# Weights of a quantised feed-forward rounded on VectorE inside an earlier stage, its input rows normalised by two engines

## What is computed

```python
# routed feed-forward, layer 0: top 3 of 64 experts, 128 places each
buf = zeros.at[fe, pos].set(xf[tok])                       # gather rows by expert
h = gelu(einsum('ecd,edh->ech', buf, w1) + b1)
y = einsum('ech,ehd->ecd', h, w2) + b2
out = zeros.at[tok].add(y[fe, pos] * gate)                 # scatter-add

# quantised feed-forward, layer 1: w_up, w_gate (768, 256), w_down (256, 768)
def lpbq_dequant(w):                                       # blocks of 32 along a row
    s = max(max|wb| / 7, 1e-12)
    return clip(round(wb / s), -8, 7) * s
x = act_qdq(x)                                             # one scale for all of x
up, gate = act_qdq(x @ dequant(w_up).T), act_qdq(x @ dequant(w_gate).T)
o = act_qdq(act_qdq(gate * fixed(sigmoid(gate))) * up)
out = o @ dequant(w_down).T
```

## Time and profile before

| | us |
|---|---|
| median of 3 runs (lowest, highest) | 2735.41 (2733.01, 2735.60) |
| the profiled execution, its own time | 2738.86 |
| its span in the profile | 2737.10 |
| mean granted clock of TensorE | 0.921 |
| DMA over the span | 339.40 MB, mean 124 GB/s |

### The profile page before, as it was taken

How to read it: one execution, slowest core, us unless ns; L and a number is a source line. 1 busy time by engine, 2 the same in 40 slices (tenths; PEclk the granted TensorE clock), 3 DMA queues, 4 the chain that set the end, 5 groups by cost and what they waited for, 6 DMA issues and landing times. The chain is left out here.

```text
span 2737.1 us, 52948 instructions
## 1 busy us (share of the span) xinstructions
PE 2340.4 (86%) x18240; PEld 1860.6 (68%) x18240; DVE 1495.7 (55%) x2887; ACT 1247.6 (46%) x2737; POOL 629.3 (23%) x690
## 2 busy tenths in 40 slices
PE   8989999877999999489948999999999997695047
PEld 5669999767999999478835666666666665353035
DVE  5766666574111111268844666565666664644865
ACT  2223323211434343168734656555555654436753
POOL 1101111155434444534431121111121110000000
PEclk9999999968999999789968999999999997798579
DMA  2122322082999999500025555555455551110111
GB/s 81 53 72 70 78 71 65 22 281 81 341 342 345 341 348 342 174 1 0 0 45 135 128 125 125 128 122 122 119 128 125 125 125 48 59 57 0 50 46 42
DMA packets 375990, 339.40 MB, mean 124 GB/s; under 512 B 70227, under 2 KB 351853, under 8 KB 374637
## 3 DMA queue, kind: packets, MB, share of 16 engines
q1 hardware_dynamic: 311148, 294.82, 36.5%
q10 hardware_dynamic: 52480, 26.83, 3.9%
q0 software_dynamic: 12288, 16.79, 2.8%
HBM read 255.03 MB, written 83.37 MB: 124 GB/s over the span
## 5 line engine op out<-in xcount | busy, mean ns | idle before, releaser
L2124 ACT COPY rel_probT<-rel_ps_t 121x400 f32<-121x400 f32 x384 | 196.4, 511 | 259.5 <-PE rel_ps_t L2356 259.5
L2136 ACT ACTIVATE rel_prob<-rel_ps_s,rel_nmx 100x361 f32<-100x361 f32 x512 | 264.9, 580 | 2.1 <-DVE rel_nmx L2238 2.1
L2356 PEld LDWEIGHTS rel_ps_t<-rel_ident,rel_prob 100*121 100x121 f32 x1536 | 197.7, 187 | 78.1 <-ACT rel_probT L2124 49.2
L2356 PE MATMUL rel_ps_t<-rel_ident,rel_prob 100*121 100x100 f32 x1536 | 244.5, 282 | 7.2 <-ACT rel_probT L2124 7.2
L1328 PEld LDWEIGHTS moe_ps_h<-moe_xeT,moe_w 128*128 128x128 f32 x2048 | 241.3, 194 | 5.1 <-issue 1.9
L1328 PE MATMUL moe_ps_h<-moe_xeT,moe_w 128*128 128x128 f32 x2048 | 241.9, 277 | 1.3 <-DVE moe_xeT L1493 1.3
L2238 DVE TENSOR_REDUCE rel_nmx<-rel_ps_s 100x2 f32<-100x722 f32 x256 | 232.8, 909 | 8.8
L1328 PE MATMUL moe_ps_y<-moe_w,moe_hT 128*128 128x256 f32 x1024 | 231.4, 379 | 0.0
L1319 ACT ACTIVATE moe_hT<-moe_ps_h,moe_b 128x128 f32<-128x128 f32 x512 | 143.0, 375 | 138.4 <-PE moe_ps_h L1328 138.0
L2876 PE MATMUL ffd_ps_y<-ffn_w_dT,ffd_oq 128*100 128x256 f32 x384 | 85.9, 385 | 140.2 <-DVE ffd_oq L2821 134.6
L1328 PEld LDWEIGHTS moe_ps_y<-moe_w,moe_hT 128*128 128x128 f32 x1024 | 189.6, 190 | 23.2
(11 more groups left out here) (430 smaller groups left out, 4946.2 us busy)
## 6 DMA issues: line engine op xcount, KB each, us to landing
moe_w<-in_L_ffn_w SPq DMA_DIRECT2D x128, 1024.0 KB
rel_scores<-rel_r_ext SPq DMA_DIRECT2D x32, 818.8 KB
rel_r_key<-rel_scores SPq DMA_DIRECT2D x32, 818.8 KB
rel_weights<-rel_prob ACTq DMA_DIRECT2D x128, 204.7 KB
rel_by_dist<-rel_weights SPq DMA_DIRECT2D x32, 400.0 KB
mut_ctx_nat<-in_ctx SPq DMA_DIRECT2D x32, 363.0 KB
mut_ctx_T<-in_ctxT SPq DMA_DIRECT2D x16, 722.0 KB
rel_ctx_T<-in_ctxT SPq DMA_DIRECT2D x32, 361.0 KB, 3.3
```

The costliest lines, as they stand in the source:

```text
L2124: nc.scalar.copy(probT[:, pg % 2, c], ps_pT).then_inc(s_t_sb, 1)
L2136: last = nc.scalar.activation(prob[:, t.parity, slot, :], ps_s[0:S, j, 0:L], ACT.Exp, bias=nmx[:, slot:slot + 1])
L2356: last = nc.tensor.transpose(ps_pT[:, j, :], prob[:, pt.parity, QUAD * pg + j, c * STEP:c * STEP + R], ident[0:S, 0:S])
```

## The change

- A new class `QuantisedAhead` owns the three weight tiles, for which memory is now held from the routed stage to the end. Its `load` puts the three loads on SP's queue at the head of the routed stage, behind `ahead.load`. Its `step` issues one of 18 instructions: six for each tile, the same operations as before, each waiting for the one before it.
- DVE's list for the experts: the loop ends at expert 42 instead of 62, the last 22 are written out, and one step follows each of experts 42 to 59.
- POOL adds the first two one-hots straight into `mask`; the tile `hot01` goes.
- Preparation stage: no loads and no quantising. DVE normalises the rows of the first three groups (12 sequences) and takes their maxima, then takes the maxima of the other five as ACT finishes them, and copies the three transposes of the down weights out of PSUM (three banks of their own) after the first three of these. ACT normalises 20 rows, written out without the loop, and copies the 8 transposes of the up and gate weights. PE makes the first four of those, then the three of the down weights, then the last four.
- `up_kept` gets its memory behind this stage.

```diff
+class QuantisedAhead:
+    STEPS = 18
...
+    def load(self, sp):
+        sp.dma_start(self.w_in[:, 0], io["L1_ffn_w_up"]...).then_inc(self.s_w[0], 16)
+        sp.dma_start(self.w_in[:, 1], io["L1_ffn_w_gate"]...).then_inc(self.s_w[1], 16)
+        sp.dma_start(self.w_d[:], io["L1_ffn_w_down"]...).then_inc(self.s_w[2], 16)
+
+    def step(self, dve, i):
+        nc, n, k = self.nc, i // 6, i % 6
+        blocks = self.flat[n].rearrange("p (b k) -> p b k", k=self.BLOCK)
+        if i > 0:
+            dve.wait_ge(self.s_q, i)
+        if k == 0:
+            dve.wait_ge(self.s_w[n], 16)
+            nc.vector.tensor_reduce(self.top[:], blocks, AX.X, ALU.max, apply_absolute_value=True).then_inc(self.s_q, 1)
...
@@ routed_ffn
             ahead.load(sp)
+            quantised.load(sp)
...
-                    nc.gpsimd.tensor_tensor(hot01[:], hot[:, v, :, 0, :], hot[:, v, :, 1, :], ALU.add).then_inc(s_hot01, 1)
+                    nc.gpsimd.tensor_tensor(mask[:, v], hot[:, v, :, 0, :], hot[:, v, :, 1, :], ALU.add).then_inc(s_hot01, 1)
                     pool.wait_ge(s_hot01, nxt.i + 1)
-                    nc.gpsimd.tensor_tensor(mask[:, v], hot01[:], hot[:, v, :, 2, :], ALU.add).then_inc(s_mask, 1)
+                    nc.gpsimd.tensor_tensor(mask[:, v], mask[:, v], hot[:, v, :, 2, :], ALU.add).then_inc(s_mask, 1)
...
-            rounds(dve, expert, -2, 2, E - 2, E, DEEP)
+            def last_expert(t):
+                expert(t)
+                if isinstance(t.i, int) and STILL <= t.i < STILL + quantised.STEPS:
+                    quantised.step(dve, t.i - STILL)
+
+            STILL = E - 2 - DEEP * 5
+            rounds(dve, last_expert, -2, 2, STILL, E, DEEP)
...
@@ quantised_ffn, preparation
-                q = Chain(dve, s_q, 15)
-                for n in range(3):
-                    dve.wait_ge(s_w[n], 16)
...
-                turns(dve, largest, 0, 0, GROUPS, GROUPS)
+                for g in range(OWN):
+                    for b in range(g * G, (g + 1) * G):
+                        nc.vector.tensor_scalar(y_nat[:, b, :], y_nat[:, b, :], mean[:, b:b + 1], rstd[:, b:b + 1],
+                                                ALU.subtract, ALU.mult).then_inc(s_own, 1)
+                for g in range(OWN):
+                    dve.wait_ge(s_own, (g + 1) * G)
+                    largest(g)
+                for g in range(OWN, GROUPS):
+                    dve.wait_ge(s_x, (g - OWN + 1) * G)
+                    largest(g)
+                    if g - OWN < IC // 2:
+                        i = g - OWN
+                        dve.wait_ge(s_d, i + 1)
+                        nc.vector.tensor_copy(w_dT[:, 2 * i:2 * i + 2, :].rearrange("p e d -> p (e d)"),
+                                              ps_d[:, i, 0:2 * D]).then_inc(s_d_sb, 1)
+                dve.wait_ge(s_d_sb, IC // 2)
...
@@ PE: the four banks, with the down weights behind the first four sets
-                    pe.wait_ge(s_wq, n + 1)
                     if i >= 4:
                         pe.wait_ge(s_t_sb, i - 3)
...
+                    if i == 3:
+                        for j, (parts, _) in enumerate(downs()):
+                            for e, tile in enumerate(parts):
+                                last = nc.tensor.transpose(ps_d[:, j, e * P:(e + 1) * P], tile, ident[:])
+                            last.then_inc(s_d, 1)
...
@@ ACT
-                with act.Fori(0, GROUPS) as g:
+                for b in range(OWN * G, B):
...
```

More of the change, by code:

```diff
@@ L1031, in causal_bias, with routed_ffn @@
                                      compare_op=ALU.is_ge, fill=low, base=0, channel_multiplier=1).then_inc(self.s_bias, 1)
-def routed_ffn(nc, io, keep, ahead):
+def routed_ffn(nc, io, keep, ahead, quantised):
     B, S, D = io["x"].shape
@@ L1074, in routed_ffn @@
         hot = m.sb("hot", [S, 2, G, TOP, E])
-        hot01 = m.sb("hot01", [S, G, E])
         mask = m.sb("mask", [S, 2, G, E])
@@ L2422, in _, with quantised_ffn @@
         nc.gpsimd.partition_all_reduce(all_top[:], top[:], parts, bass.bass_isa.ReduceOp.max).then_inc(s_all, 1)
-def quantised_ffn(nc, io, keep, out):
+def quantised_ffn(nc, io, keep, out, ahead):
     B, S, D = io["x"].shape
     I = io["L1_ffn_w_up"].shape[0]
-    BLOCK = 32
     KC, IC = D // P, I // P
@@ L2455, in quantised_ffn @@
         with ExitStack() as ctx:
[L2457 to L2465, removed]
+            m = Names(nc, ctx, "ffx")
+            w_in, w_d = ahead.w_in, ahead.w_d
             row_top = m.sb("row_top", [S, GROUPS])
@@ L2468, in quantised_ffn @@
             ps = m.ps("ps", [P, 4, 512])
[L2469 to L2472, removed]
+            ps_d = m.ps("ps_d", [P, 3, 512])
+            s_const, s_t, s_t_sb, s_d, s_d_sb = (m.sem(n) for n in (
+                "constants", "in_transposed", "in_stored", "down_transposed", "down_stored"))
+            s_shift, s_x, s_own, s_top = m.sem("shift"), m.sem("rows_normalised"), m.sem("own_rows_normalised"), m.sem("row_maxima")
             block = ctx.enter_context(nc.Block())
[L2475 to L2479, removed]
+            OWN = 3
             @block.gpsimd
@@ L2526, in _ @@
                 pe.wait_ge(s_const, 2)
-                for i, (n, tiles, _) in enumerate(transposes()):
-                    pe.wait_ge(s_wq, n + 1)
+                for i, (tiles, _) in enumerate(inputs()):
                     if i >= 4:
@@ L2537, in _ @@
                 act.wait_ge(s_shift, 1)
-                with act.Fori(0, GROUPS) as g:
-                    for q in range(G):
-                        b = g * G + q
-                        nc.scalar.activation(at(y_nat, b), at(y_nat, b), ACT.Identity, bias=shift[:, bass.ds(b, 1)],
-                                             scale=rstd[:, bass.ds(b, 1)]).then_inc(s_x, 1)
-                for i, (n, tiles, out) in enumerate(transposes()):
+                for b in range(OWN * G, B):
+                    nc.scalar.activation(y_nat[:, b, :], y_nat[:, b, :], ACT.Identity, bias=shift[:, b:b + 1],
+                                         scale=rstd[:, b:b + 1]).then_inc(s_x, 1)
+                for i, (tiles, out) in enumerate(inputs()):
                     act.wait_ge(s_t, i + 1)
@@ L2899, in bass_decoder @@
             mutual_attention(nc, io, keep, ahead)
[L2900 to L2905 removed]
+        with ExitStack() as of_quantised:
+            quantised = QuantisedAhead(nc, of_quantised, io)
+            with ExitStack() as of_causal:
+                ahead = CausalAhead(nc, of_causal, io)
+                routed_ffn(nc, io, keep, ahead, quantised)
+                causal_heads(nc, io, keep, ahead)
+            relative_cross(nc, io, keep)
+            quantised_ffn(nc, io, keep, out, quantised)
 _TRANSPOSED = {"L0_attn_WvT": "L0_attn_Wv", "L0_xattn_WvT_s": "L0_xattn_Wv_s", "L0_xattn_WvT_c": "L0_xattn_Wv_c",
```

75 lines of the change are left out of this document (47 added, 28 removed).

## The result

The changed kernel took **2721.69 us** (median of 5 runs, 2716.78 to 2725.69); before, on the same chip, 2735.41 (5 runs, 2731.53 to 2737.12). The ratio is 0.9949 with a 95% interval of 0.9934 to 0.9963: faster, by 0.5%, since the interval does not reach 1. The profiled execution took 2725.69 us with a span of 2723.6, against 2738.86 and 2737.10.

A forecast was written before the change was run, and what follows sets the result against it. Bound stage by stage: DVE ends the preparation, PE paces the experts, DVE and the DMA queue the routing. -19.6 + 6.5 + 0.7 = -12.4 us, giving 2723.0 us for the median; range 2714 to 2731.

The forecast's parts named there:

- Preparation stage, -19.6: Quantised feed-forward's preparation: without weight wait and quantising, DVE reaches its last reduction at 2338.1 instead of 2357.71, -19.6 us.
- The quantising among the experts, 0: Experts 42 to 59: 18 DVE steps, at most 1.76 us each, fit 5.6 us of slack under PE's pace; cost 0.
- The three loads, +6.5: Head of the routed stage: 2.36 MB of weight loads delay the row stores DVE waits for; +6.5 us, bounds 0 and 7.1.
- My own sign of being wrong: Prediction called wrong if routing ended as early as before or over 10 us later; first expert's transposes expected at about 664.5.
- the gaps before 579 (0.04 of 25 us) give 1 us at most: Routing: the DMA queue, at share 0.96 from 554 on, could absorb at most 1 us of the three loads.
- any lateness of that store is lateness of DVE: Routing: DVE stood 3.64 us at 578.82 for a row store, so delaying that store was taken to delay DVE equally.
- Rival 1: Routing absorbs the three loads in queue gaps or DVE catches up later: -18.9 us, 2716.5 us; chance 0.16.
- Rival 2: Routing: loads cost 13.8 us instead of 6.5, through issues and PE's lower clock in two more groups: 2730.3 us; chance 0.13.
- Nothing is won back before the experts: Routing after the third store wait: DVE works through remaining groups at its own pace, 9.6 us to the next group.
- End barrier, +0.7: Kernel end: the new owner of the weight semaphores adds one clearing and one barrier, +0.7 us.
- TensorE's clock, 0: Stage behind the preparation: PE idles 5 us instead of 10 ahead of it; clock gain taken as 0, -3 kept for range.
- The rule weighed: Experts: DVE and GpSimd lock a shared port pair, so a 1.76 us step becomes at most 3.4 us; sum unchanged.

The follow-up runs named there:

- e_own0: Changed kernel with ACT normalising all 32 rows of the preparation stage, DVE none: 2727.84 us, ratio to the kernel before 0.9979.
- e_pad2: Changed kernel with two extra maxima of a weight tile, results unused, behind each of the 18 quantising steps: 2718.09 us (one run).
- e_pad4: Changed kernel with four extra maxima of a weight tile, results unused, behind each of the 18 quantising steps: 2759.27 us (one run).
- e_quant_back: Changed kernel with all 18 quantising steps moved back to the head of the preparation stage: 2744.88 us, ratio to the kernel before 1.0038.
- c_after: The changed kernel as it is, run again in another set of runs: 2723.07 us, ratio to the kernel before 0.9964.
- e_more_bytes: Changed kernel with two experts' first weights (2.1 MB) also loaded at the head of the routed stage, ahead of the row stores: 2726.55 us (one run).
- e_zeros_late: Changed kernel with the three weight loads and the 3.28 MB store of zeros issued behind the last routing group's rows: 2721.52 us, ratio to before 0.9958.

## Why the prediction was right, and where it was not

The time, 2723.0 predicted and 2721.69 measured, is right within the scatter of the runs. The largest term is right by its mechanism; that the sum came out this near is partly luck, for a term too large by 3 to 4.5 us stands in it against one of 5 to 6 that is missing.

- *Preparation stage, -19.6*: measured -19.8. The parts as well: 12 rows 3.96 (4.0), copies 0.69 each, 0.6 back to back, four maxima 4.60, last reduction 14.9 us behind the shift (15). ACT ends 0.9 us before DVE (0.6). e_own0 shows why the division matters, 3.7 us.
- *The quantising among the experts, 0*: right, and its slack nearly: 5.3 us are free in e_pad2, and e_pad4 puts the edge at 6.0 where I had 5.6. The cover is PE's 7.25 us an expert; without it the price is 21 us (e_quant_back).
- *The three loads, +6.5*: **this step failed in its size.** The routing became 2.1 us longer in the profiled pair; in seven executions with the loads at its head it took 110.1 to 114.7 (median 110.5) against 107.5 to 109.7 in three before, and 107.0 to 107.2 in three with the loads late. The term is thus 2 to 3.5 us (in c_after, with its lower clock at the end, the routing is 5 to 7 longer), and the first expert's transposes stood at 657.64, not at 664.5. My own sign of being wrong, a routing that ends as early as before, was met in time from the span's start (657.96 before), since the stage began 2.5 us sooner; only its length shows the 2.1 us. The step "the gaps before 579 (0.04 of 25 us) give 1 us at most" is what was wrong, twice. First, I took the share of 0.96 at 311 GB/s as a full queue, but it went to 352 GB/s with the loads in it, over 25 us, so 41 x 25 = 1 MB or 2.9 us at that rate came out of what looked like no gap. Second, "any lateness of that store is lateness of DVE" forgot POOL: DVE's four rows at 565.21 took 1.38 us behind their wait, where those at 563.99 before took 2.34 beside POOL. DVE's waits grew by 3.91 + 3.47 - 3.64 = 3.7 us, and 1.0 of that was saved in the rows. 3.7 - 1.0 = 2.7, which agrees with the 2.6 more between first rows and third. Rival 1, that the routing absorbs the loads, was half right: it absorbed more than half of them. e_more_bytes shows the other half of it, in one execution: behind the first 2.36 MB nothing is absorbed. Rival 2 was priced on a misread row: the granted clock over the products of the earlier trace rows is 0.54, not 0.50, and at 1.00 they take 2.92 us, which is 2.3 less, not 2.6.
- *"Nothing is won back before the experts"*: true of the pair shown (578.63 to the first transposes is 79.0 us, before 578.82 to 657.96 is 79.1). But a gain at the head of the routing is not simply passed on either: in e_zeros_late the last products ran at the lower clock and took the 2 us back.
- *End barrier, +0.7*: the barriers are 13 instead of 12. From the last reduction to the end it is 379.4 us before and 380.0 after, but this stretch is 379.4 to 380.5 in the three profiles of the kernel before and 378.2 to 380.7 in the eleven of changed versions, so the term is too small to be seen.
- *TensorE's clock, 0*: right; the next stage's head again runs at 0.50 (1.2 GHz) over 2347 to 2355, though PE's idle stretch ahead of it is 5.07 us instead of 9.86.
- *The rule weighed* (the Trainium skill, SBUF — State Buffer, Who interferes with whom). I let the lock make a step of 1.76 at most 3.4 us. DVE's step kept its 1.75; it was POOL's scatter that grew, by 0.57 us, and only beside the two-input multiplications. The Trainium skill has the second comer wait there, and that is POOL here: its scatter starts at 1044.02, when the step still has 0.69 us to run (1042.96 + 1.75 - 1044.02). So the trace agrees with the rule in who waits and nearly in how long, and I had applied it to the wrong engine. The step with one input at 1021.23 overlapped the scatter as much and left it at 1.60; the rounding (L1027) had ended before the scatter began, so it says nothing. The sum was indeed not touched, since POOL has time in an expert.
- *Cross attention*: no step of the prediction looked at it. Of memory it said only "The kept up projections get their memory later: no instruction", among the edits at nothing, and I had read the holding of three tiles as a matter of room in the same way. If what is held is the cause, which stays open, it costs 5 to 6 us, and that makes up for what the loads did not cost.

Summed for the changed kernel from many profiles: -19.8, +2 to +3.5 for the loads, up to +0.7 at the end and about +6 in the cross attention, about -12 to -9.5; the ratios of the three timed pairs (0.9949, 0.9964, 0.9955) are -14.0, -9.8 and -12.3 us of 2735.

## What to carry to other kernels

A step of a busy engine moved into another stage is free up to the moment at which the waiting successor is needed, not only up to the end of its idle gap: add the gap and the successor's own slack, keep below the engine's whole idle time in a turn, and pad the step on the chip to find the edge. A DMA share of 0.96 does not mean that added bytes wait in full; the first ones cost less than half their time here in six of seven executions, and the next ones all of it in the one that was tried. Holding memory and semaphores across stages changes what all stages between are given, so compare the stages that a change does not touch as well.

## What I had not expected of the chip

- The DMA engines moved 381 GB/s over 551 to 569 with loads and stores mixed in the queue (the second window above), while the three loads alone ran at 334.
- Where DVE's two-input multiplication of 128x1536 and POOL's issue of an indirect DMA met, POOL, which came second, was held up (1.60 to 2.17 us), not DVE (1.75).
- The last 24 products of the routing took 2.92 us at a granted clock of 1.00 in ten of the fourteen profiles, but 4.97 at 0.56 (near the level of 1.2 GHz) in e_zeros_late, where they began early, and 4.81 at 0.59 in c_after, where they began late. A stage can win or lose 2 us by this alone.
- The wait for one DMA of 400 KB in a stage that was not touched was about 35 us in sum in some kernels and 46 in others, in the same program text; the cause is open.
